# First expert layer of a two-layer network: second products in split f32 instead of f32

## The chip, the cores and the metric

The kernel runs on one core of one Trainium2 chip. The metric is the device time of one execution in microseconds, the median of a few runs. One core has five engines with instruction streams of their own: TensorE (PE; its weight loads are shown as PEld), VectorE (DVE), ScalarE (ACT), GpSimd (POOL) and SyncE (SP, which here only starts DMAs). They order themselves by semaphores.

## The reference

The input is 4 sequences of 1024 rows of 256 numbers, 4096 rows in all. Two layers follow, each an attention-like part and a layer of experts, each added to its input:

```
x = x + L0_attn(layernorm(x))     # gated recurrent scan
x = x + L0_ffn(layernorm(x))      # 8 experts, the best 2 for each row   <- the change is here
x = x + L1_attn(layernorm(x))     # 16 heads, causal softmax
x = x + L1_ffn(layernorm(x))      # 32 experts, the best 4 for each row, and a shared one
```

The first expert layer, for one row x and each of its two experts e, with H = 512:

```
scores = gate_w @ x;  p = softmax(the best two scores)
h1, h2 = w12[e] @ x, split in halves of H
y     += p[e] * (w3[e] @ (silu(h1) * h2))
```

## The kernel before

The program passes four stages: the scan, the first expert layer, the attention, the second expert layer. The change touches the second one.

There, each row has been normalised and written to a DRAM table `routed0` at a place of its expert, so that 128 rows that follow each other there form a tile with one expert. There are TILES0 = 71 tiles at most (4096 x 2 / 128 + 7), and the number of the expert of tile n is found at run time and lies in `b_tei[0, n]`. An engine that needs it for an address reads it into a register first (`value_load`).

The weights of the first products, w12, are held twice: as `b_w12h`, rounded to f32r (a shorter form of f32 that TensorE multiplies in one pass), and `b_w12l`, the rest, also f32r. A product of two such pairs is made as three f32r products (high x high, high x low, low x high) added up in PSUM. The weights of the second products, w3, are held once, in plain f32, for all experts: `b_w3T`.

For tile n the engines do this, in each engine's own order:

- SP (`load_tile`, L655 to L659) loads the tile's rows to `b_xt[j]`, j = n mod 2, once VectorE has made the gates `b_wt` of tile n-2 (s_btk).
- TensorE (`tile_products`) for tile n: `hidden(n, c=0)`, six f32r matmuls with 512 columns into one PSUM bank (L2343 to L2345); `transpose_hidden(n-1)`, four transposes of the gated rows (L2351); `hidden(n, c=1)`, six more; `transpose_rows(n+1)`, two transposes of the next tile's rows (L2332); `second_layer(n-1)`, four f32 matmuls of 128x256, which the trace shows as eight instructions (L2360). So the second products of a tile come one tile late. `hidden(n, 0)` waits for VectorE's low part of the transposed rows (s_btl); `second_layer(n)` for ScalarE's copy of the transposed gated rows (s_bhT) and for the PSUM bank of y (s_bye).
- ScalarE (`tile_step`): `tanh_half(n)` (L1124), `take_hidden(n-1)`, the copy of the gated transposed rows from PSUM (L1128), `take_rows(n+1)`, the high part of the next rows (L1120), `take_y(n-1)`, y times the gate to a ring of four buffers `b_y` (L1137).
- VectorE (`tile_step`): the first gating product (L1726), the second (L1729), `low_rows(n+1)`, the low part of the next rows (L1719), and three small instructions that make the gate (L1737 to L1741).
- GpSimd (`add_rows`): the scatter-add of b_y to DRAM (L888), which waits until the one before has landed.

The order within an engine is fixed by the program; an engine waits at an instruction whose semaphores are not there yet, and all behind it wait too. The next stage starts when all 71 scatter-adds have landed.

Two rows of the trace come from other lines: L1068 and L1571 make `b_w12h` and `b_w12l` (128x1024 at a time) ahead of the tile loop, and L2827 and L2838 are f32r products of the last stage, with 256 columns. L512 is a `value_load` ahead of a DMA (L513), once for each of eight experts, half of them on ScalarE.

Of the kernel before, what the change touches and what calls it, by code (L numbers as in the profile page):

```python
# [5 lines left out]
F32 = mybir.dt.float32  # L6
F32R = mybir.dt.float32r
# [3 lines left out]
ALU = mybir.AluOpType  # L11
ACT = mybir.ActivationFunctionType
AX_X = mybir.AxisListType.X

P = 128
# [30 lines left out]
def network(nc, x_in, a_params, w12T, w3T, gate0T, wqkT, wvT, woT, swT, bias1, ewT, out):  # L46
    B, S, D = x_in.shape
# [3 lines left out]
    E0 = gate0T.shape[2]  # L51
# [10 lines left out]
    KH = H0 // P  # L62
    HT = 2 * H0 // P
    REGION = T + P
    TILES0 = T * K0 // P + E0 - 1
# [20 lines left out]
    with ExitStack() as ctx:  # L86
# [3 lines left out]
        def sem(name):  # L90
            return ctx.enter_context(nc.semaphore(name))
# [28 lines left out]
        def place(name, shape, dt=F32):  # L120
            n = 2 if dt == BF16 else 4
            for s in shape[1:]:
                n *= s
            t = nc.alloc_sbuf_tensor_at(name, shape, dt, offset=at[0])
            at[0] += (n + 31) // 32 * 32
            assert at[0] <= arena_end, (name, at[0] - arena_end)
            return t
# [9 lines left out]
        PS = ctx.enter_context(nc.psum_tensor("PS", [P, 8, 512], F32))  # L137
# [5 lines left out]
        b_w3T = place("b_w3T", [P, KH, E0 * D])  # L143
# [43 lines left out]
        b_tT = [place(f"b_tT{n}", [P, 2, KD, P], F32R) for n in ("_hi", "_lo")]  # L187
        b_sg = place("b_sg", [P, 2, H0])
        b_hid = place("b_hid", [P, 2, H0])
        b_hT = place("b_hT", [P, 2, KH, P])  # L190
        b_y = place("b_y", [P, BY, D])
        b_tok = place("b_tok", [P, BY], U32)
        b_wt = place("b_wt", [P, BY])
# [31 lines left out]
        b_tt = place("b_tt", [P, TILES0])  # L225
        b_tei = place("b_tei", [P, TILES0], I32)
        b_rowi = place("b_rowi", [P, TILES0], I32)

        BLOCKS = [(c, j) for c in range(NC2) for j in range(4 * (c + 1))]
        CHUNKS = [(t, c) for t in range(QT) for c in range(t // 4 + 1)]  # L230
# [147 lines left out]
        s_bhid = sem("b_gated_ready")  # L378
        s_bht = sem("b_gated_transposed")
        s_bhT = sem("b_gatedT_ready")  # L380
        s_by = sem("b_y_ready")
        s_bye = sem("b_y_taken")
        s_xs = sem("x1_stored")
# [139 lines left out]
        def finish_stage(eng, n):  # L523

            leave_stage(eng)
            enter_stage(eng, n)
# [475 lines left out]
        def _(act):  # L1002
# [115 lines left out]
            def take_rows(n, j):  # L1118
                act.wait_ge(s_btt, n + 3)
                act.activation(b_tT[0][:, j, :, :].rearrange("p k t -> p (k t)"), PS[:, 4, 0:D], ACT.Copy).then_inc(s_btT, 1)  # L1120
# [4 lines left out]

            def take_hidden(n, j):
                act.wait_ge(s_bht, n + 1)
                act.activation(b_hT[:, j, :, :].rearrange("p k t -> p (k t)"), PS[:, 5, :], ACT.Copy).then_inc(s_bhT, 1)  # L1128

            def take_y(n, r):  # L1130
                act.wait_ge(s_by, n + 1)
                act.wait_ge(s_btk, n + 3)

                if not (isinstance(n, int) and n < BY):
                    act.wait_ge(s_bst, n * 16 - 16 * (BY - 1))
                act.sem_inc(s_pass, 1)
                act.activation(b_y[:, r, :], PS[:, 6 + r % 2, 0:D], ACT.Identity, bias=zeros[:, 0:1],  # L1137
                               scale=b_wt[:, r:r + 1]).then_inc(s_bye, 1)

            def tile_step(n, r):  # L1140
                tanh_half(n, r % 2)
                take_hidden(n - 1, 1 - r % 2)
                if not (isinstance(n, int) and n == TILES0 - 1):
                    take_rows(n + 1, 1 - r % 2)
                take_y(n - 1, (r - 1) % BY)

            take_rows(0, 0)
            tanh_half(0, 0)
            take_rows(1, 1)
            for n in range(1, BY + 1):  # L1150
                tile_step(n, n % BY)
                if n <= ZERO_PARTS:
                    part = T // ZERO_PARTS
                    act.dma_start(acc[0][(n - 1) * part:n * part, :].rearrange("(q p) d -> p q d", p=P),
                                  zeros[:, :].rearrange("p (a d) -> p a d", a=1).broadcast_to([P, part // P, D])).then_inc(s_dax, 16)
# [327 lines left out]
        def _(dve):  # L1483
# [232 lines left out]
            def low_rows(n, j):  # L1716
# [2 lines left out]
                dve.tensor_tensor(b_tT[1][:, j, :, :].rearrange("p k t -> p (k t)"), PS[:, 4, 0:D],  # L1719
                                  b_tT[0][:, j, :, :].rearrange("p k t -> p (k t)").bitcast(F32), ALU.subtract).then_inc(s_btl, 1)  # L1720

            def tile_step(n, r):
                j = r % 2

                dve.wait_ge(s_bsg, n + 1)
                st.done(dve.scalar_tensor_tensor(b_hid[:, j, :], b_sg[:, j, :], 1.0, PS[:, 2 * j, :], ALU.add, ALU.mult))  # L1726
                st.sync()
                dve.wait_ge(s_bh2, n + 1)
                dve.scalar_tensor_tensor(b_hid[:, j, :], b_hid[:, j, :], 0.5, PS[:, 2 * j + 1, :], ALU.mult,  # L1729
                                         ALU.mult).then_inc(s_bhid, 1)  # L1730
                if not (isinstance(n, int) and n == TILES0 - 1):
                    low_rows(n + 1, 1 - j)

                if not (isinstance(n, int) and n < BY):
                    dve.wait_ge(s_bst, n * 16 - 16 * (BY - 1))
                    dve.sem_inc(s_pass, 1)
                st.done(dve.tensor_copy(b_tok[:, r:r + 1], b_xt[:, j, TOK:TOK + 1].bitcast(U32)))  # L1737
                st.done(dve.tensor_scalar(b_wt[:, r:r + 1], b_xt[:, j, FIRST:FIRST + 1], b_te[:, bass.ds(n, 1)], b_xt[:, j, GAP:GAP + 1],
                                          ALU.is_equal, ALU.mult))
                st.sync()  # L1740
                dve.tensor_tensor(b_wt[:, r:r + 1], b_wt[:, r:r + 1], b_xt[:, j, SECOND:SECOND + 1], ALU.add).then_inc(s_btk, 1)  # L1741
# [10 lines left out]
                st.end()  # L1752
            for n in range((TILES0 // BY - 1) * BY, TILES0):
                tile_step(n, n % BY)
            finish_stage(dve, 1)

            def moments(g):
# [453 lines left out]
        def _(pe):  # L2211
# [111 lines left out]
            def expert_of(n):  # L2323
                return pe.value_load(b_tei[0:1, bass.ds(n, 1)], min_val=0, max_val=E0 - 1)
# [26 lines left out]
                    ins = pe.transpose(PS[:, 5, k * P:(k + 1) * P], b_hid[:, j, k * P:(k + 1) * P], ident[:, :])  # L2351
                ins.then_inc(s_bht, 1)

            def second_layer(n, j, e):
                pe.wait_ge(s_bhT, n + 1)

                pe.wait_ge(s_bye, n + 1)
                pe.sem_inc(s_pass, 1)
                for k in range(KH):
                    ins = pe.matmul(PS[:, 6 + j, 0:D], b_hT[:, j, k, :], b_w3T[:, k, bass.ds(e * D, D)],  # L2360
                                    start=(k == 0), stop=(k == KH - 1))
                ins.then_inc(s_by, 1)

            transpose_rows(0, 0, 0)
            pe.wait_ge(s_wdl, E0 + LO_DVE)
            pe.wait_ge(s_wpl, E0 - LO_DVE)
            pe.wait_ge(s_bw3, 16 * KH)
            e = expert_of(0)
            for c in range(2):
                hidden(0, 0, c, e)  # L2370
# [1 line left out]
            def tile_products(n, half, j):  # L2372
                e = expert_of(n)
                hidden(n, j, 0, e)
                transpose_hidden(n - 1, 1 - j)
                hidden(n, j, 1, e)
                if half:
                    transpose_rows(n + 1, *half, 1 - j)
                second_layer(n - 1, 1 - j, expert_of(n - 1))

            LOOPS = (TILES0 - 2) // 2
            with pe.Fori(0, LOOPS) as i:
# [3 lines left out]
                tile_products(n, ((n + 1) // 2,) if n + 1 < TILES0 else (), n % 2)  # L2386
            last = TILES0 - 1
            transpose_hidden(last, last % 2)
            second_layer(last, last % 2, expert_of(last))
            finish_stage(pe, 1)  # L2390

            pe.sem_inc(s_cPu, 2 * ROUND)
# [522 lines left out]
```

## Time and profile before

| | us |
|---|---|
| median of 3 runs | 2140.64 (2138.8 to 2143.95) |
| the profiled execution: its time | 2142.65 |
| its span in the trace | 2140.9 |
| mean granted clock of TensorE | 0.941 |
| busy: PE / PEld / DVE / ACT / POOL | 1889.4 / 1430.0 / 1361.5 / 1079.1 / 1177.9 |
| the tile loop of this layer, by its first and last tanh | 192.7 to 559.1 |

A row of a group of instructions gives the source line, the engine, the operation, what is written <- what is read, the count, and times. In a timeline the first two numbers are the start and the length in us, and a bracket at the end is the idle time of the engine before it and what ended it. Matmul ends are modelled; weight loads show better when the next matmul is taken up.

### The profile page before, as it was taken

What the parts mean: (1) busy time and instruction counts of PE and PEld (TensorE: products, weight loads), DVE (VectorE), ACT (ScalarE), POOL (GpSimd) and SP (SyncE); (2) the same over time, 40 slices, a digit from 0 to 9 for tenths busy, and PEclk for the clock granted to TensorE, in tenths of its full rate; (3) what the DMA queues carried; (4) which work ended last, traced back from release to release, by engine and by line L of the source; (5) the groups of instructions that cost most, each with busy time, mean ns of one, the idle gap of its engine ahead of it and who ended that gap; (6) DMA issues with size and microseconds to landing.
All of it is one profiled execution on the core that took longest, in us unless ns stands there. A gap on an engine that the chain in (4) does not pass through costs nothing. (4 is left out here: it accounts for less than half of the span.)

```text
span 2140.9 us, 39708 instructions
## 1 busy us (share of the span) xinstructions
PE 1889.4 (88%) x12071; PEld 1430.0 (67%) x12072; DVE 1361.5 (64%) x3652; ACT 1079.1 (50%) x2250; POOL 1177.9 (55%) x1159
## 2 busy tenths in 40 slices
PE   5864999999589999999999999999999999973870
PEld 3553888888466677777777677777777777753750
DVE  7884334434467777657777656777656777653763
ACT  5331333333455556646655646655646655522760
POOL 4364223223216666636687836687836687835782
PEclk9856999999899999999999999999999999977995
DMA  9853433333332111111221111121112111122979
GB/s 335 268 188 119 89 52 49 52 52 49 77 92 56 53 55 49 54 32 53 54 77 41 48 33 53 51 53 47 48 27 59 48 52 51 39 94 70 205 129 257
DMA packets 215682, 177.33 MB, mean 83 GB/s; under 512 B 85442, under 2 KB 200727, under 8 KB 214880
## 3 DMA queue, kind: packets, MB, share of 16 engines
q1 hardware_dynamic: 177904, 138.78, 22.1%
q0 software_dynamic: 28656, 27.61, 8.4%
q10 hardware_dynamic: 8960, 8.92, 1.2%
q8 instruction: 84, 1.38, 0.3%
q14 instruction: 78, 0.64, 0.1%
HBM read 95.05 MB, written 80.72 MB: 82 GB/s over the span
## 5 line engine op out<-in xcount | busy, mean ns | idle before, releaser
L952 POOL TENSOR_TENSOR c_den_late<-c_den_late,c_p 128x512 f32<-128x512 f32 (+3 forms) x384 | 409.9, 1068 | 227.6 <-ACT c_p L1267 183.5
L1267 ACT ACTIVATE c_p<-PS 128x512 f32<-128x512 f32 (+3 forms) x768 | 343.6, 491 | 196.1 <-PE PS L2483 119.0
L2452 PE MATMUL PS<-c_k,c_q 128*128 128x512 f32 (+2 forms) x768 | 289.3, 377 | 18.1 <-DVE c_max L1838 6.7
L2495 PE MATMUL PS<-c_p,c_vh 128*64 128x256 f32 (+3 forms) x3072 | 292.5, 333 | 0.0
L2475 PE MATMUL PS<-c_q,c_k 128*128 128x512 f32 (+2 forms) x768 | 283.7, 373 | 1.8 <-DMA c_q<-c_mr 1.2
L888 POOL DMA_INDIRECT acc<-b_y,b_tok x71 | 110.5, 1557 | 272.8 <-ACT b_y L1137 241.7
L2495 PEld LDWEIGHTS PS<-c_p,c_vh 128*64 128x64 f32 x3072 | 194.6, 137 | 96.0 <-issue 38.1
L2476 PE MATMUL PS<-c_q,c_k 128*128 128x512 f32 (+2 forms) x768 | 258.4, 348 | 0.0
L1258 ACT ACTIVATE c_q<-PS 64x512 fp32r<-64x512 f32 x256 | 151.0, 590 | 208.6 <-PE PS L2439 205.4
L1845 DVE CUSTOM_DVE_ANT_0 PS<-PS,c_maskq,c_max 128x128 f32<-128x128 f32 (+3 forms) x256 | 143.1, 559 | 105.5 <-PE PS L2452 71.5
L1838 DVE TENSOR_REDUCE c_max<-PS 128x1 f32<-128x512 f32 x256 | 175.5, 685 | 54.2 <-PE PS L2452 53.6
L2452 PEld LDWEIGHTS PS<-c_k,c_q 128*128 128x128 f32 x768 | 145.7, 190 | 96.0 <-DVE c_max L1845 40.8
L952 POOL TENSOR_TENSOR c_den<-c_den,c_p 128x384 f32<-128x384 f32 (+2 forms) x192 | 141.5, 737 | 113.7 <-ACT c_p L1267 88.6
L1845 DVE CUSTOM_DVE_ANT_0 PS<-PS,c_maskq 128x128 f32<-128x128 f32 (+3 forms) x256 | 125.9, 501 | 114.5 <-PE PS L2452 109.8
L921 POOL DMA_INDIRECT routed<-r_rows,r_slot x128 | 128.5, 1004 | 60.7 <-DVEq L1956 33.4
L1726 DVE SCALAR_TENSOR_TENSOR b_hid<-b_sg,PS 128x512 f32<-128x512 f32 x71 | 48.9, 689 | 176.1 <-ACT b_sg L1124 176.1
L2475 PEld LDWEIGHTS PS<-c_q,c_k 128*128 128x128 f32 x768 | 145.2, 189 | 16.7 <-DMA c_q<-c_mr 1.3
L2476 PEld LDWEIGHTS PS<-c_q,c_k 128*128 128x128 f32 x768 | 145.1, 189 | 9.0
L2360 PE MATMUL PS<-b_w3T,b_hT 128*128 x568 | 134.8, 380 | 2.7 <-issue 1.7
L2343 PE MATMUL PS<-b_w12h,b_tT_hi 128*128 x284 | 129.2, 455 | 2.3 <-DVE b_tT_lo L1719 2.3
L2522 PE MATMUL PS<-c_wo,c_yT 128*128 128x256 f32 x512 | 124.6, 387 | 0.0
L991 POOL DMA_INDIRECT acc<-d_y,d_tok x64 | 100.5, 1571 | 38.4 <-ACT d_y L1446 20.7
(304 smaller groups left out, 4009.7 us busy)
## 6 DMA issues: line engine op xcount, KB each, us to landing
c_vh<-c_v SPq DMA_DIRECT2D x64, 256.0 KB, 3.2
c_rrow<-rden SPq DMA_DIRECT2D x63, 256.0 KB, 3.6
routed<-b_empty SPq DMA_DIRECT2D x32, 289.0 KB, 10.2
d_xe<-routed SPq DMA_DIRECT2D x32, 289.0 KB, 4.0
b_xt<-routed SPq DMA_DIRECT2D x71, 130.0 KB, 2.1
b_w12T<-in_w12T_dram SPq DMA_DIRECT2D x16, 512.0 KB, 13.9
d_acc<-acc SPq DMA_DIRECT2D x16, 512.0 KB, 9.0
c_st_hi<-wqk_split SPq DMA_DIRECT2D x48, 128.0 KB
```

Of the source, the lines that this page charges most:

```text
L921: pool.indirect_dma_start(routed1, bass.IndirectOffsetOnAxis(ap=r_slot[n][:, j // K1, j % K1:j % K1 + 1], axis=0), r_rows[n][:, j // K1, : ...
L952: pool.tensor_tensor(den[:, off:], den[:, off:], p, ALU.add).then_inc(s_cPa, 1)
L1258: act.activation(dst, src, ACT.Copy).then_inc(s_cqs, 1)
L1267: act.activation(c_p[:, P_AT[h][m]:P_AT[h][m] + WIDTH[m]], PS[:, ST_BANK[m % STB], skip:skip + WIDTH[m]], ACT.Exp, scale=ATT_SCALE).then_i ...
L1838: dve.tensor_reduce(dst, src, AX_X, ALU.max).then_inc(s_turn[bank], 1)
L1845: dve.tensor_tensor_reduce(src, src, c_maskq[:, 512 - w:512], 1.0, dst if c else BIG, ALU.add, ALU.max, dst).then_inc(s_turn[bank], 1)
L2343: pe.matmul(PS[:, 2 * j + c, :], b_tT[0][:, j, k, :], b_w12h[k][:, cols], start=(k == 0), stop=False)
L2360: ins = pe.matmul(PS[:, 6 + j, 0:D], b_hT[:, j, k, :], b_w3T[:, k, bass.ds(e * D, D)], start=(k == 0), stop=(k == KH - 1))
L2452: pe.matmul(PS[:, 2 + use[0], 0:max(w, 256)], c_q1[h][:, t * P:(t + 1) * P], c_k1[h][:, c * 512:c * 512 + max(w, 256)], start=True, stop=T ...
L2475: pe.matmul(PS[:, bank, 0:n], c_k1[h][:, j * P:(j + 1) * P], c_q1[h][:, q], start=True, stop=False)
L2476: ins = pe.matmul(PS[:, bank, 0:n], c_k2[h][:, j * P:(j + 1) * P], c_q2[h][:, q], start=False, stop=not diagonal)
L2495: ins = pe.matmul(dst, c_vh[h][:, j, :], columns[:, :, a, :], start=(j == 0), stop=(t0 == 3))
```

## The change

- A second pair of buffers, `b_w3` (high, low), holds the w3 of one tile's expert in split form; there is one pair, not two. ScalarE makes the high part tile by tile (`high_second`), in its order between `take_rows(n+1)` and `take_y(n-1)`; VectorE makes the low part (`low_second`), at the head of its `tile_step`. Both read the expert's number for themselves.
- The gated transposed rows `b_hT` are split too: ScalarE's copy now rounds to f32r, and VectorE subtracts (`low_hidden`) after its first gating product. There was one f32 buffer for each j; now there is one high and one low for all tiles.
- `second_layer` makes twelve f32r matmuls instead of four f32 ones: eight with the high rows and both weights, then a wait for the low rows, then four with the low rows and the high weights. It no longer reads the expert's number.
- The wait for the loading of w3 moves from TensorE to ScalarE.

```diff
-        b_hT = place("b_hT", [P, 2, KH, P])
+        b_hT = [place(f"b_hT{n}", [P, KH, P], F32R) for n in ("_hi", "_lo")]
...
+        b_w3 = [place(f"b_w3{n}", [P, KH, D], F32R) for n in ("_hi", "_lo")]
...
             def take_hidden(n, j):
                 act.wait_ge(s_bht, n + 1)
-                act.activation(b_hT[:, j, :, :].rearrange("p k t -> p (k t)"), PS[:, 5, :], ACT.Copy).then_inc(s_bhT, 1)
+                act.activation(b_hT[0][:, :, :].rearrange("p k t -> p (k t)"), PS[:, 5, :], ACT.Copy).then_inc(s_bhT, 1)
+
+            def high_second(n):
+
+                if not (isinstance(n, int) and n == 0):
+                    act.wait_ge(s_by, n)
+                e = act.value_load(b_tei[0:1, bass.ds(n, 1)], min_val=0, max_val=E0 - 1)
+                act.activation(b_w3[0][:, :, :], b_w3T[:, :, bass.ds(e * D, D)], ACT.Copy).then_inc(s_w3h, 1)
...
                     take_rows(n + 1, 1 - r % 2)
+                high_second(n)
                 take_y(n - 1, (r - 1) % BY)

+            act.wait_ge(s_bplan, 2)
+            act.wait_ge(s_bw3, 16 * KH)
             take_rows(0, 0)
             tanh_half(0, 0)
             take_rows(1, 1)
+            high_second(0)
...
+            def low_second(n):
+
+                dve.wait_ge(s_w3h, n + 1)
+                e = dve.value_load(b_tei[0:1, bass.ds(n, 1)], min_val=0, max_val=E0 - 1)
+                dve.tensor_tensor(b_w3[1][:, :, :], b_w3T[:, :, bass.ds(e * D, D)], b_w3[0][:, :, :].bitcast(F32),
+                                  ALU.subtract).then_inc(s_w3l, 1)
+
+            def low_hidden(n):
+
+                dve.wait_ge(s_bhT, n + 1)
+                dve.tensor_tensor(b_hT[1][:, :, :].rearrange("p k t -> p (k t)"), PS[:, 5, :],
+                                  b_hT[0][:, :, :].rearrange("p k t -> p (k t)").bitcast(F32), ALU.subtract).then_inc(s_bhl, 1)
+
             def tile_step(n, r):
                 j = r % 2

+                if not (isinstance(n, int) and n == 0):
+                    low_second(n - 1)
                 dve.wait_ge(s_bsg, n + 1)
                 st.done(dve.scalar_tensor_tensor(b_hid[:, j, :], b_sg[:, j, :], 1.0, PS[:, 2 * j, :], ALU.add, ALU.mult))
+                if not (isinstance(n, int) and n == 0):
+                    low_hidden(n - 1)
                 st.sync()
...
-            def second_layer(n, j, e):
+            def second_layer(n, j):
                 pe.wait_ge(s_bhT, n + 1)
+                pe.wait_ge(s_w3l, n + 1)

                 pe.wait_ge(s_bye, n + 1)
                 pe.sem_inc(s_pass, 1)
                 for k in range(KH):
-                    ins = pe.matmul(PS[:, 6 + j, 0:D], b_hT[:, j, k, :], b_w3T[:, k, bass.ds(e * D, D)],
-                                    start=(k == 0), stop=(k == KH - 1))
+                    for w in range(2):
+                        pe.matmul(PS[:, 6 + j, 0:D], b_hT[0][:, k, :], b_w3[w][:, k, :], start=(k == 0 and w == 0), stop=False)
+                pe.wait_ge(s_bhl, n + 1)
+                for k in range(KH):
+                    ins = pe.matmul(PS[:, 6 + j, 0:D], b_hT[1][:, k, :], b_w3[0][:, k, :], start=False, stop=(k == KH - 1))
                 ins.then_inc(s_by, 1)
```

## Rows read from the trace of the kernel before

**Rows 1.** Stretches in us: busy by engine (instructions), granted clock, DMA share, GB/s.
```profile
core 0: us, PE busy (x) PEld busy (x) DVE busy (x) ACT busy (x) POOL busy (x), PEclk, DMA share, GB/s
120.00:180.00 60.00, 25.07 (x167) 22.59 (x167) 48.96 (x232) 19.80 (x25) 40.43 (x38) 0.50 0.43 147
...
400.00:500.00 100.00, 100.00 (x504) 83.18 (x503) 41.22 (x118) 39.07 (x77) 29.80 (x20) 1.00 0.33 51
2040.00:2060.00 20.00, 16.66 (x96) 12.97 (x95) 13.13 (x39) 13.85 (x31) 16.61 (x12) 0.91 0.89 180
2060.00:2080.00 20.00, 15.83 (x112) 13.82 (x110) 15.09 (x43) 14.25 (x33) 16.90 (x11) 1.00 0.65 73
```

**Rows 2.** Waits from 200 to 560 us: who <- whom, us in total, times, longest.
```profile
DVE b_hid L1726 <- ACT b_sg L1124: 170.0, 69, 3.6
...
PEld PS L2343 <- issue: 3.9, 18, 0.2
```

**Rows 3.** Timeline of one tile in the loop, all engines, some lines of it.
```profile
401.95 0.19 PEld L2343 LDWEIGHTS PS<-b_w12h,b_tT_hi 128*128 128x128 f32 x1
...
403.32 0.59 PEld L2351 LDWEIGHTS PS<-ident,b_hid 128*128 128x128 f32 x4
...
403.75 0.60 ACT L1124 ACTIVATE b_sg<-PS 128x512 f32<-128x512 f32 x1 [0.65 <-PE PS L2345]
...
403.87 0.19 PEld L2343 LDWEIGHTS PS<-b_w12h,b_tT_hi 128*128 128x128 f32 x1
...
404.38 0.69 DVE L1726 SCALAR_TENSOR_TENSOR b_hid<-b_sg,PS 128x512 f32<-128x512 f32 x1 [2.42 <-ACT b_sg L1124]
...
405.48 1.60 PEld L2360 LDWEIGHTS PS<-b_w3T,b_hT 128*128 128x128 f32 x8
...
405.76 0.69 DVE L1729 SCALAR_TENSOR_TENSOR b_hid<-b_hid,PS 128x512 f32<-128x512 f32 x1 [0.69 <-PE PS L2345]
...
406.36 0.42 DVE L1719 TENSOR_TENSOR b_tT_lo<-PS,b_tT_hi 128x256 fp32r<-128x256 f32 x1
...
407.21 0.19 PEld L2343 LDWEIGHTS PS<-b_w12h,b_tT_hi 128*128 128x128 f32 x1
...
407.68 0.57 ACT L1137 ACTIVATE b_y<-PS,zeros,b_wt 128x256 f32<-128x256 f32 x1 [1.51 <-DMA acc<-b_y,b_tok]
```

**Rows 4.** The tanh's line: ns min/median/max, first and last start.
```profile
L1124 ACT ACTIVATE b_sg<-PS x71: 597/597/599, 192.7 to 559.1; 128x512 f32<-128x512 f32 x71
```

**Rows 5.** Timeline of PE alone, last stage, around two groups of L2838.
```profile
2062.57 0.28 PE L2838 MATMUL PS<-d_wf,d_eh_lo 128*128 128x256 f32 x1
...
2062.81 0.28 PE L2838 MATMUL PS<-d_wf,d_eh_lo 128*128 128x256 f32 x1
...
2065.01 0.39 PE L2838 MATMUL PS<-d_wf,d_eh_hi 128*128 128x256 f32 x1 [0.53 <-DVE d_eh_lo L2184]
...
2065.47 0.28 PE L2838 MATMUL PS<-d_wf,d_eh_lo 128*128 128x256 f32 x1
```

**Rows 6.** Lines that do such conversions elsewhere: ns min/median/max, first and last start.
```profile
L1068 ACT ACTIVATE b_w12h<-b_w12T x16: 1039/1043/1047, 126.2 to 157.8; 128x1024 fp32r<-128x1024 f32 x16
...
L1571 DVE TENSOR_TENSOR b_w12l<-b_w12T,b_w12h x14: 1217/1224/1226, 128.1 to 174.7; 128x1024 fp32r<-128x1024 f32 x14
...
L1808 DVE TENSOR_TENSOR c_xT_lo<-PS,c_xT_hi x16: 680/692/693, 588.5 to 1547.5; 128x512 fp32r<-128x512 f32 x16
```

**Rows 7.** Register reads on ScalarE's queue and the DMA issues behind them, same columns.
```profile
L512 ACTq TENSOR_LOAD <-b_zrowi x4: 279/382/542, 159.9 to 163.4; - x4
...
L512 ACTq FUSED_REGOPS  x4: 152/157/170, 160.4 to 164.0; - x4
...
L513 ACTq DMA_DIRECT2D routed<-b_tail x4: 343/353/451, 160.8 to 164.3; - x4
```

**Rows 8.** The page's DMA issues (KB, us to landing), and the last scatter-adds in GpSimd's timeline.
```profile
b_xt<-routed SPq DMA_DIRECT2D x71, 130.0 KB, 2.1
...
565.06 1.55 POOL L888 DMA_INDIRECT acc<-b_y,b_tok  x1 [4.23 <-DMA acc<-b_y,b_tok]
569.71 1.55 POOL L888 DMA_INDIRECT acc<-b_y,b_tok  x1 [3.10 <-DMA acc<-b_y,b_tok]
```

More of the change, by code:

```diff
@@ L380, in network @@
         s_bhT = sem("b_gatedT_ready")
+        s_bhl = sem("b_gatedT_lo_ready")
+        s_w3h = sem("b_second_weights_hi_ready")
+        s_w3l = sem("b_second_weights_lo_ready")
         s_by = sem("b_y_ready")
@@ L1754, in _ @@
                 tile_step(n, n % BY)
+            low_second(TILES0 - 1)
+            low_hidden(TILES0 - 1)
             finish_stage(dve, 1)
@@ L2366, in _ @@
             pe.wait_ge(s_wpl, E0 - LO_DVE)
-            pe.wait_ge(s_bw3, 16 * KH)
             e = expert_of(0)
@@ L2378, in tile_products @@
                     transpose_rows(n + 1, *half, 1 - j)
-                second_layer(n - 1, 1 - j, expert_of(n - 1))
+                second_layer(n - 1, 1 - j)
             LOOPS = (TILES0 - 2) // 2
@@ L2388, in _ @@
             transpose_hidden(last, last % 2)
-            second_layer(last, last % 2, expert_of(last))
+            second_layer(last, last % 2)
             finish_stage(pe, 1)
```

## The prediction

> **What bounds the kernel now.** I read the table by stretches first. In the tile loop of the first expert layer TensorE is busy 100.00 of 100.00 us (400 to 500) at a granted clock of 1.00, VectorE 41%, ScalarE 39%, GpSimd 30% [rows 1]. A busy PE can still be a waiting one, because the ends of matmuls are modelled, so next come the waits: in 360 us PE's own largest wait there is 3.9 us of "issue", while VectorE waits 170.0 us for ScalarE's tanh, which itself waits for PE's products [rows 2]. Last the timeline of one tile [rows 3], where the starts of the weight loads (PEld) give PE's true pace: 1.37 us for the six products of a first half (401.95 to 403.32), 0.55 for four transposes, 1.61 for the second half and two transposes of the next rows, and 1.73 for the eight matmuls of the second layer (405.48 to 407.21), together 5.26 us with no hole. The line of the tanh gives the mean period: 71 starts from 192.7 to 559.1, so 366.4/70 = 5.23 us [rows 4]. PE's instruction stream bounds this stage: what shortens the stream is worth its full size times 71, until something else is late.
>
> **Part one: the products.** Eight f32 matmuls (four blocks, each two instructions) become twelve in f32r of the same 128x256. The last stage of this kernel has this very kind of product, f32r halves of 256 columns at clock 1.00: they start every 0.12 us (2062.57, then 2062.81 two on) [rows 5]. 12 x 0.12 = 1.44 us against 1.73: 0.29 us less per tile. PE would need 5.26 - 0.29 = 4.97 us, or 4.94 beside the mean period. It also drops one of its two reads of the expert's number per tile, which now lie under matmuls: nothing.
>
> **Part two: new work beside PE.** ScalarE gets a copy of 128x1024 to f32r from on-chip memory; the same copy takes 1.043 us in L1068. VectorE gets a subtraction of 128x1024, 1.224 us in L1571, and one of 128x512 out of PSUM, 0.69 us in L1808 [rows 6]. As load that would fit: in 5.23 us ScalarE works 0.39 x 5.23 = 2.0, then 3.1; VectorE 2.2, then 4.1. Neither is the bound by its sum. What matters is order.
>
> **Part three: the waits added.** The split pair b_w3 has one buffer. So high_second(n) waits until y(n-1) has been computed, and y(n) waits for the split. Between the two nothing overlaps: the change makes a ring, and its round is the tile's period if it is longer than PE's stream. I add it up from the end of y(n-1):
>
> 1. ScalarE sees the end, reads the expert's number into a register and starts the copy. The trace shows such a read on this engine four times: the load takes 0.279 to 0.542 us, the register operations behind it 0.157, and from the first load to the first DMA issue that uses it 0.9 us pass (159.9 to 160.8), from the last one too (163.4 to 164.3) [rows 7]. With the median load of 0.382, not 0.54, it is 0.75. A hop between engines costs 0.03 (the tanh ends at 403.75 + 0.60 = 404.35, VectorE starts at 404.38) [rows 3]. I take 0.80 in all. The bounds: nothing, if the sequencer could do it ahead of the wait (it stands behind the wait in program order, which speaks against), and 1.17, the spacing of those four loads with a DMA issue in between (3.5/3).
> 2. The copy: 1.04. Sum 1.84.
> 3. VectorE: low_second waits for the copy and then reads the number itself: 0.80 again, same bounds. Sum 2.64.
> 4. Its subtraction: 1.22, but the next instruction may start about 0.08 before the end (L1729 and L1719 start 0.60 apart, the first being 0.69 long) [rows 3]: 1.14. Sum 3.78.
> 5. Behind it in VectorE's queue stands the first gating product of tile n+1: 0.61. Sum 4.39. Its input, the tanh, stands behind the copy and take_y(n-1) on ScalarE: 1.84 + 0.57 + 0.60 = 3.0, in time [rows 3].
> 6. low_hidden(n), the low part of the gated rows: 0.69. Sum 5.08. The high part is ready at about 3.6.
> 7. PE's last four matmuls wait for it: in the last stage four such after a wait on VectorE run from 2065.01 to 2065.47 + 0.28 = 2065.75, so 0.74, and 0.04 for the hop [rows 5]. Sum 5.86 us, and y(n) is done.
>
> The first eight products can start when the low weights are there (3.86) and end before 5.08: hidden. PE's stream of the next tile is late next: low_rows(n+2) ends at 5.08 + 0.61 + 0.38 = 6.07, PE starts the next tile there, 0.21 after y(n), and reaches the second layer 3.53 later, at 3.74 of its round, 0.12 before the weights. So the ring decides, narrowly ahead of PE's own way.
>
> Other edits and movements: take_y(n-1) now stands behind the copy on ScalarE, so the scatter-add on GpSimd starts some 1.9 us later in its round. Its own chain, each add waiting for the landing of the one before, can run at 4.65 us (565.06 to 569.71, where only the landing held it) [rows 8]; below 5.86, so it costs nothing but would hold a faster loop. SP's load of tile n+2 waits for VectorE's b_wt, later by as much as the round: its rows land 2.1 us after issue [rows 8], and PE asks for them about 3.2 us (12 products of 0.23 and four transposes) after starting a tile; covered by about half a microsecond, and if not, PE waits that much, most of it under the ring. The waits for the plan and the weights, moved ahead of the loop on ScalarE, are over by then: zero. Outside this stage nothing changes; the stages behind it start later by the same amount, since the next one needs the sums of all scatter-adds.
>
> **The sum.** 5.86 against 5.23: 0.63 x 70 = 44 us, plus the last tile, which has no next tile on PE beside it: its y follows the one before after 5.25 us of the ring (5.86 less step 5) instead of about 3 (transposes 0.55, a copy of some 0.6, matmuls 1.73), +2. So 46 us. The profiled run took 2142.65 us (span 2140.9 and 1.75 around it), which gives 2188.7; it lies 2.0 above the median of 2140.64, so on the scale of the medians I forecast 2187.
>
> For the size of a register read there is a stated figure. The trace has loads of 0.279 to 0.542 us, and 0.9 until the value is used [rows 7]. The Trainium skill, "DMA: Bandwidth & Descriptors", section "Latency and other measured facts", puts the floor of a `tensor_load` at about 600 ns; an estimate with 0.6 in place of both 0.80 gives 5.46 us a round and 2159 us.
>
> **The rivals.**
> - PE stays the bound, the kernel gets faster. The conversions would have to fit beside the stream. The ring falls below 5.23 when the two reads together cost under 0.97 us instead of 1.60; with reads of no cost it is 4.26, and PE's 4.94 decides: 0.29 x 71 = 21 us less, 2120. For it: PE is the bound now without doubt, and both engines are under half busy [rows 1]. Against it: the wait stands ahead of the read in both queues. 8%.
> - The ring just equals the old period, between 5.17 and 5.29: no difference. 3%.
> - The reads are dear on these engines, 1.17 each: 6.60 us a round, 1.37 x 70 = 96, 2237. The upper ends of the loads speak for a piece of that, their median against. 8%.
> - The clock falls. PE now idles about 0.9 us in 5.86. In 120 to 180 us, where it was busy 25.07 of 60, it was granted 0.50; in the last stage 16.66 of 20 us went with 0.91 and 15.83 of 20 with 1.00 [rows 1]. PE will be busy 4.94/5.86 = 84%, as there. At half speed its stream takes 9.9 us; if a tenth of the tiles ran so, 7 x 4.0 = 28 us more, 2215. 4%.
>
> "TensorE: Matmul & The Clock Gate" of the Trainium skill, section "HAM oscillation — how this bites in real kernels", says that frequent small idle times of TensorE can make its clock swing between the two levels; the stretches of the last stage, with such holes, show 0.91 and 1.00, so it is borne out a little.
>
> **Numbers.** Forecast, a ring of 5.4 to 6.3 us: 77%. Its own range is what reads of 0.6 to 1.0 us give: 5.46 (+16 to +18) to 6.26 (+74), so 2158 to 2215. Outside lie the faster case with the even one (11%) and the dear end; I set 2157 to 2218. A difference of under 0.2% (4 us) can't be told from none here. Slower: 77 + 8 + 4 = 89, less 1 for a ring that falls short: 88%. Same 3%, faster 9%.
>
> **What would show it.** Right: the second layer's products in twelve, 0.12 us apart, with a PE wait before them for VectorE (low weights) and before the last four (low gated rows); the copy on ScalarE waiting for PE each tile; a period near 5.9 of the tanh; PE under 90% in the loop. Step 1 or 3 is wrong if from the end of y to the copy, or from the copy to the subtraction, much other than 0.8 us pass. The whole is wrong if PE stays at 100% there, or if the clock leaves 1.00.

## The result, and the profile after

The changed kernel takes 2201.89 us (median of 4 runs, 2196.72 to 2203.03), the kernel before 2139.78 on the same chip (4 runs): a ratio of 1.028, 95% interval 1.026 to 1.029; the medians are 62 us apart. The forecast was 2187, with a range of 2157 to 2218. By their own profiled executions the two are 2201.86 and 2142.65, a difference of 59.2 us.

A stretch of the tile loop, in the columns of [rows 1]:

```profile
400.00:500.00 100.00, 89.47 (x499) 72.23 (x497) 63.69 (x136) 47.75 (x82) 38.62 (x17) 1.00 0.28 43
```

TensorE fell from 100% to 89%, VectorE rose from 41% to 64%, ScalarE from 39% to 48%; the clock stayed at 1.00. No engine is full any more: that is the look of a ring of waits. Its stations are in the list of waits from 240 to 600 us, about 60 tiles, against [rows 2]:

```profile
DVE b_w_lo L1741 <- ACT b_w_hi L1139: 131.4, 59, 2.3
ACT b_w_hi L1139 <- PE PS L2399: 131.1, 60, 2.6
...
PEld PS L2377 <- issue: 48.7, 60, 1.1
PE PS L2377 <- DVE b_tT_lo L1734: 36.8, 60, 0.9
...
PEld PS L2399 <- DVE b_hT_lo L1747: 5.2, 30, 0.2
```

ScalarE's copy waits in every tile for the last products of the tile before (L2399), VectorE's subtraction in every tile for the copy. In the timeline (start, length) one round can be followed line by line, against [rows 3]:

```profile
408.38 0.74 PE L2399 MATMUL PS<-b_w_hi,b_hT_lo 128*128 128x256 f32 x4
408.84 0.41 DVE L1734 TENSOR_TENSOR b_tT_lo<-PS,b_tT_hi 128x256 fp32r<-128x256 f32 x1
...
409.54 0.19 PEld L2377 LDWEIGHTS PS<-b_w12h,b_tT_hi 128*128 128x128 f32 x1 [0.62 <-issue]
...
410.02 1.06 ACT L1139 ACTIVATE b_w_hi<-b_w3T 128x1024 fp32r x1 [2.02 <-PE PS L2399]
...
411.95 1.23 DVE L1741 TENSOR_TENSOR b_w_lo<-b_w3T,b_w_hi 128x1024 fp32r<-128x1024 f32 x1 [2.25 <-ACT b_w_hi L1139]
```

y ends at 408.38 + 0.74 = 409.12; the copy starts at 410.02, 0.90 later, and ends at 411.08; the subtraction starts 0.87 later, at 411.95. The rest of the same round:

```profile
413.09 0.68 DVE L1756 SCALAR_TENSOR_TENSOR b_hid<-b_sg,PS 128x512 f32<-128x512 f32 x1
413.69 0.68 DVE L1747 TENSOR_TENSOR b_hT_lo<-PS,b_hT_hi 128x512 fp32r<-128x512 f32 x1
414.42 0.74 PE L2399 MATMUL PS<-b_w_hi,b_hT_lo 128*128 128x256 f32 x4
```

So y ends next at 415.16: a round of 6.04 us. The tanh gives the mean, against [rows 4], and three lines with the register reads stand against [rows 7]:

```profile
L1128 ACT ACTIVATE b_sg<-PS x71: 585/597/602, 193.6 to 615.9; 128x512 f32<-128x512 f32 x71
...
L1138 ACTq TENSOR_LOAD <-b_tei x71: 275/428/510, 196.5 to 619.6; - x71
...
L1740 DVEq TENSOR_LOAD <-b_tei x71: 299/305/1062, 198.3 to 621.8; - x71
...
L2358 PEldq TENSOR_LOAD <-b_tei x71: 298/308/491, 188.9 to 612.9; - x71
```

422.3/70 = 6.03 us a tile against 5.23: 0.80 x 70 = 56 us, and the other 3 of the 59.2 us are lost at the two ends of the loop.

### The profile page after: what moved, and what is told of

Same layout as the page of the kernel before. It is cut to its first block and busy times, and to the rows that moved or that the text cites. A ratio compares the mean times of both kernels' runs of the same rounds, so it can differ in the third digit from the quotient of the medians.

```text
span 2200.1 us, 40735 instructions
## 1 busy us (share of the span) xinstructions
PE 1906.8 (87%) x12355; PEld 1433.6 (65%) x12356; DVE 1478.7 (67%) x3795; ACT 1143.3 (52%) x2322; POOL 1224.2 (56%) x1159
## 5 line engine op out<-in xcount | busy, mean ns | idle before, releaser
L892 POOL DMA_INDIRECT acc<-b_y,b_tok x71 | 155.8, 2194 | 285.4 <-ACT b_y L1148 269.2
L1741 DVE TENSOR_TENSOR b_w_lo<-b_w3T,b_w_hi 128x1024 fp32r<-128x1024 f32 x71 | 87.0, 1225 | 159.9 <-ACT b_w_hi L1139 144.8
L1139 ACT ACTIVATE b_w_hi<-b_w3T 128x1024 fp32r x71 | 75.3, 1060 | 155.9 <-PE PS L2399 151.9
```

The costliest lines, as they stand in the source:

```text
L892: pool.indirect_dma_start(acc0, bass.IndirectOffsetOnAxis(ap=b_tok[:, r:r + 1], axis=0), b_y[:, r, :], None, compute_op=ALU.add).then_inc( ...
```

## The experiments

The runs of this section were made on three chips, on which the kernel before takes 2141.2, 2155.5 and 2156.2 us, so ratios to the kernel before are compared. The theory: the ring y, read, copy, read, subtraction, gating, low rows, last products. The rivals: the load of VectorE and ScalarE as such; the late start of TensorE's tiles; the new products themselves.

**Both reads ahead of their waits.** The number of the expert doesn't depend on what the two engines wait for.

```diff
             def high_second(n):
-                if not (isinstance(n, int) and n == 0):
-                    act.wait_ge(s_by, n)
                 e = act.value_load(b_tei[0:1, bass.ds(n, 1)], min_val=0, max_val=E0 - 1)
+                if not (isinstance(n, int) and n == 0):
+                    act.wait_ge(s_by, n)
             def low_second(n):
-                dve.wait_ge(s_w3h, n + 1)
                 e = dve.value_load(b_tei[0:1, bass.ds(n, 1)], min_val=0, max_val=E0 - 1)
+                dve.wait_ge(s_w3h, n + 1)
```

> The changed kernel, with the register reads of the expert's number on ScalarE and VectorE each put ahead of the wait behind which they stood; nothing else differs. Ring theory: in the changed kernel's trace the round of 6.03 us contains 0.92 us from the end of y to the copy on ScalarE and 0.84 us from the copy to the subtraction on VectorE, nearly all of it the two reads. With the reads in waiting time the ring falls to about 4.4 us, PE's own stream decides at 4.95 to 5.25 us a tile, and the time is 2125 to 2150, so not slower than the kernel before (2139.8). Load theory (VectorE and ScalarE simply have more to do, or TensorE's starts are late because of the low rows): where the reads stand makes no difference, 2195 to 2203.

Measured: 2139.56 us, ratio 0.999 (0.998 to 1.000). Moving two lines gives back the whole loss, as expected. In its timeline:

```profile
402.43 0.54 PEld L2399 LDWEIGHTS PS<-b_w_hi,b_hT_lo 128*128 128x128 f32 x4
402.95 0.19 PEld L2377 LDWEIGHTS PS<-b_w12h,b_tT_hi 128*128 128x128 f32 x1
403.31 1.06 ACT L1139 ACTIVATE b_w_hi<-b_w3T 128x1024 fp32r x1 [1.13 <-PE PS L2399]
...
404.52 1.23 DVE L1741 TENSOR_TENSOR b_w_lo<-b_w3T,b_w_hi 128x1024 fp32r<-128x1024 f32 x1 [1.41 <-ACT b_w_hi L1139]
...
407.34 0.54 PEld L2399 LDWEIGHTS PS<-b_w_hi,b_hT_lo 128*128 128x128 f32 x4
...
408.58 0.19 PEld L2377 LDWEIGHTS PS<-b_w12h,b_tT_hi 128*128 128x128 f32 x1 [0.69 <-issue]
```

With 0.74 for the last products, y ends at about 403.17; the copy follows after 0.14 instead of 0.90, the subtraction after 0.15 (404.37 to 404.52) instead of 0.87. The reads were nearly all of these two gaps. The load theory is out: both engines do the same work in less time. And a new thing shows: every second tile TensorE begins 1.24 us after the start of the last four weight loads, not 0.52.

**One read at a time.** The same edit on one engine alone.

> The changed kernel with only ScalarE's read ahead of its wait. Ring theory: 6.03 - 0.85 = 5.2 us a tile, 58 us less than the changed kernel, 2140 to 2150. Load theory: 2195 to 2203.

> The changed kernel with only VectorE's read ahead of its wait. Ring theory: 6.03 - 0.78 = 5.25 us a tile, 55 us less than the changed kernel, 2142 to 2152. Load theory: 2195 to 2203. If only one of this run and the one with ScalarE's read gains, that side alone was the late one and there is no ring.

Measured: 2172.32 us, ratio 1.014 (1.012 to 1.016), and 2162.18 us, ratio 1.009 (1.008 to 1.011). Both gain, so there is a ring through both engines, but 0.014 and 0.019 below the changed kernel's 1.028 are only 30 and 40 us, half to three quarters of the 58 and 55 that were expected. Both expectations missed. The waits of the first of the two from 240 to 560 us point at TensorE:

```profile
PEld PS L2377 <- issue: 28.9, 29, 1.1
PE PS L2377 <- DVE b_tT_lo L1734: 23.1, 29, 0.9
```

29 waits in 57 tiles, 1 us each: in every second tile TensorE is late with its own start. The expectations had left TensorE's own way out. Whether it makes up the whole of the missing 28 and 15 us was not tested by itself.

**The suspected cost doubled.**

```diff
+                act.value_load(b_tei[0:1, bass.ds(n, 1)], min_val=0, max_val=E0 - 1)
                 e = act.value_load(b_tei[0:1, bass.ds(n, 1)], min_val=0, max_val=E0 - 1)
```

> The changed kernel with the read on ScalarE made twice in a row behind its wait, the first one's value not used: the suspected cost doubled on one side. ScalarE is busy only half the time. Ring theory: the second read lengthens the round by the 0.5 to 0.8 us that a read takes, 35 to 56 us more than the changed kernel, 2237 to 2258. Load theory: ScalarE hides it, 2200 to 2206.

Measured: 2236.45 us, ratio 1.044 (1.042 to 1.046): 0.016, some 34 us, or 0.5 us a tile, on an engine that is busy 44% of the time. This is the low end of what was expected (2237). The second of the two reads in a row is a load of 0.278 us at the median, with 0.152 and 0.018 of register work behind it:

```profile
L1139 ACTq TENSOR_LOAD <-b_tei x71: 272/278/287, 193.7 to 654.3; - x71
```

**TensorE's read and branch ahead.** In the changed kernel TensorE starts a tile 0.42 us (409.12 to 409.54) after y, every second one 0.8 after:

```profile
402.36 0.73 PE L2399 MATMUL PS<-b_w_hi,b_hT_lo 128*128 128x256 f32 x4
...
403.87 0.19 PEld L2377 LDWEIGHTS PS<-b_w12h,b_tT_hi 128*128 128x128 f32 x1 [0.98 <-issue]
```

If this late start were the loss, putting the read and the branch ahead of the second layer should give it back. The matmuls keep their order; the loop is cut at another place.

```diff
             def tile_products(n, half, j):
                 e = expert_of(n)
+                if not (isinstance(n, int) and n == 1):
+                    second_layer(n - 2, j)
                 hidden(n, j, 0, e)
...
                     transpose_rows(n + 1, *half, 1 - j)
-                second_layer(n - 1, 1 - j)
```

> The changed kernel with only TensorE's read and branch ahead of the second layer; the reads on ScalarE and VectorE stay behind their waits. TensorE waits 0.4 to 0.8 us at the start of each tile in the changed kernel. Ring theory: that wait lies under the ring, which does not pass through it; 6.0 us a tile as before, 2196 to 2205. Rival (the late start of TensorE's tile is the loss): 0.6 us a tile less, about 2160.

Measured: 2214.30 us against 2155.5, ratio 1.027 (1.025 to 1.029): nothing, as the ring theory expected. The trace shows that the edit took away only a part of the late start:

```profile
401.02 0.42 DVE L1734 TENSOR_TENSOR b_tT_lo<-PS,b_tT_hi 128x256 fp32r<-128x256 f32 x1
401.72 0.19 PEld L2377 LDWEIGHTS PS<-b_w12h,b_tT_hi 128*128 128x128 f32 x1 [0.50 <-issue]
...
407.04 0.42 DVE L1734 TENSOR_TENSOR b_tT_lo<-PS,b_tT_hi 128x256 fp32r<-128x256 f32 x1
407.74 0.19 PEld L2377 LDWEIGHTS PS<-b_w12h,b_tT_hi 128*128 128x128 f32 x1 [0.63 <-issue]
```

Here every tile starts 0.28 to 0.29 us after VectorE has ended the low part of the next rows (L1734), which is 0.3 to 0.4 after y. In the changed kernel the tiles that start at 0.42 have the same 0.28 to 0.29 (408.84 + 0.41 = 409.25, start at 409.54), and the others 0.60 to 0.73. TensorE's queue shows what is different in those, for the tiles that start at 409.54 and at 416.02:

```profile
L2358 PEldq TENSOR_LOAD <-b_tei x2: 307/340/373, 408.5 to 415.0; - x2
...
L2358 PEldq SEQ_ASSERT  x2: 18/18/18, 409.1 to 415.6; - x2
...
L2419 PEldq COMPARE_BRANCH  x1: 207/207/207, 414.5 to 414.5; - x1
```

Without the branch the read is over at 409.1, before the low part of the next rows, so the read costs nothing and those rows decide. With the branch ahead of it the read is over at 415.6, later than the rows (414.88 + 0.41 = 415.29). So the late start has two causes: the next rows in all tiles, and branch and read on top in every second one. Only the second was removed here, about 0.2 us a tile on average, which would be some 13 us or a ratio of 1.022 if it counted. The late start lies under the ring, as long as there is one.

**All three reads ahead.**

> The kernel of the run with both reads ahead, and on TensorE the read of the next tile's expert number and the loop's branch put ahead of the second layer's products (the same matmuls in the same order; only the loop is cut at another place). In that run's trace every other tile starts on TensorE about 0.5 us after y instead of 0.2 before its end, because the wait for the low gated rows holds the sequencer, and the branch and the read come behind it (about 1.3 us after the low rows, 1.6 with the branch). If that is so, these tiles lose nothing now: about 0.3 us a tile on average, 4.9 to 5.0 us, 2114 to 2124, faster than the kernel before by about 1%. If the late start is due to the low part of the next rows instead, nothing changes: 2136 to 2143.

Measured: 2167.01 us against 2155.5, ratio 1.005 (1.003 to 1.006): not the gain of 1%, but worse than with two reads ahead. TensorE's weight loads in its timeline:

```profile
403.74 0.38 PEld L2366 LDWEIGHTS PS<-ident,b_xt 128*128 128x128 f32 x2
404.08 0.19 PEld L2396 LDWEIGHTS PS<-b_w_hi,b_hT_hi 128*128 128x128 f32 x1
...
405.91 0.19 PEld L2377 LDWEIGHTS PS<-b_w12h,b_tT_hi 128*128 128x128 f32 x1 [0.34 <-issue]
...
409.01 0.37 PEld L2366 LDWEIGHTS PS<-ident,b_xt 128*128 128x128 f32 x2
409.87 0.19 PEld L2396 LDWEIGHTS PS<-b_w_hi,b_hT_hi 128*128 128x128 f32 x1 [0.49 <-issue]
```

Without the branch the second layer follows the transposes by 0.34, with it by 0.86. Branch and read had only changed their place: where they stand now a read is covered, but not a read and a branch. And at 405.91 TensorE waited for the low part of the next rows (VectorE's L1734 ended at 405.21 + 0.41 = 405.62, 0.29 before), though the profile books it as "issue". So each of the two causes that the expectation had as rivals was half of it.

**No tile by tile split.** The weights of expert 0 are split once ahead of the loop.

```diff
-                high_second(n)
                 take_y(n - 1, (r - 1) % BY)
...
-                if not (isinstance(n, int) and n == 0):
+                if isinstance(n, int) and n == 1:
                     low_second(n - 1)
```

> The changed kernel without the tile by tile split of the second weights: those of expert 0 are split once ahead of the loop and used for all tiles (so the part left out is the other experts' second weights, and the output differs). The twelve f32r products and the split of the gated rows stay. Ring theory: no wait of this kind is left, TensorE's stream decides at 4.95 us plus the exposed branch and read on every other tile, 5.0 to 5.25 a tile, 2120 to 2141. Rival (twelve products instead of eight, or the low gated rows, cost the time): the time stays above 2180. GpSimd's scatter-adds take 2.27 us in the changed kernel instead of 1.555; if VectorE's subtraction from and to on-chip memory beside them is the reason, they are back at 1.56 here.

Measured: 2148.72 us against 2155.5, ratio 0.996 (0.995 to 0.997). The twelve products and the split of the gated rows are no loss: the rival is out. Its tanh runs from 207.3 to 566.7, 5.13 us a tile. That mean holds one odd tile at the start, which this edit makes by itself: TensorE waits there for the one split.

```profile
212.60 1.23 DVE L1740 TENSOR_TENSOR b_w_lo<-b_w3T,b_w_hi 128x1024 fp32r<-128x1024 f32 x1 [1.46 <-issue]
...
215.08 0.29 PEld L2375 LDWEIGHTS PS<-b_w12h,b_tT_hi 128*128 128x128 f32 x1 [5.54 <-issue]
```

From the first tanh to the second 10.74 us pass, and behind that wait the granted clock was 0.72 over 216 to 222, so the lower level for a part of it. Soon after, the tiles take 4.9 and 5.14 to 5.26 in turn. And the scatter-adds are short again (changed kernel first, then this run):

```profile
L892 POOL DMA_INDIRECT acc<-b_y,b_tok x71: 1555/2270/2566, 205.7 to 628.4; - x71
```

```profile
L892 POOL DMA_INDIRECT acc<-b_y,b_tok x71: 1555/1555/1627, 223.7 to 576.1; - x71
```

**Two buffers for the high weights.** Another way to open the ring, with the reads left where they were.

```diff
-                if not (isinstance(n, int) and n == 0):
-                    act.wait_ge(s_by, n)
+                if not (isinstance(n, int) and n <= 1):
+                    act.wait_ge(s_by, n - 1)
...
                 dve.wait_ge(s_w3h, n + 1)
+                if not (isinstance(n, int) and n == 0):
+                    dve.wait_ge(s_by, n)
```

> The changed kernel with two buffers for the high part of the split weights (the low part keeps one); ScalarE's copy for tile n now waits for y(n-2), VectorE's subtraction for the copy and for y(n-1). No read is moved. Ring theory: the first 1.95 us of the round (ScalarE's read and copy) fall out, the rest of it is 4.1 us, TensorE decides with its exposed read and branch: 5.2 to 5.5 us a tile, 2135 to 2160. Rival (where the buffers are doesn't matter, the load does): 2195 to 2205.

Measured: 2161.75 us against 2155.5, ratio 1.003 (1.002 to 1.004), which is 2146 on the scale of the expectation (2139.8). The copy is off the ring and nearly all of the loss is gone. Two buffers for both parts were not tried.

**The low gated rows first on VectorE.**

```diff
                     low_second(n - 1)
+                    low_hidden(n - 1)
                 dve.wait_ge(s_bsg, n + 1)
                 st.done(dve.scalar_tensor_tensor(b_hid[:, j, :], b_sg[:, j, :], 1.0, PS[:, 2 * j, :], ALU.add, ALU.mult))
-                if not (isinstance(n, int) and n == 0):
-                    low_hidden(n - 1)
```

> The changed kernel with one order changed on VectorE: the low part of the gated rows (low_hidden) right behind the subtraction of the weights, ahead of the first gating product of the next tile. Simple reading of the ring: the gating product (0.6 us) leaves it, 5.4 us a tile, ratio to the kernel before about 1.008. Ring theory with TensorE's own way close behind it: all that VectorE does up to the low part of the next rows ends no earlier (6.14 us after y in the changed kernel's trace), TensorE starts 0.29 later, needs 3.44 to the second layer and 1.7 for it, 11.57 us for two tiles, 5.8 a tile: ratio 1.018 to 1.024. The changed kernel has 1.028.

Measured: 2206.02 us against 2156.2, ratio 1.023 (1.022 to 1.025). The second way of reckoning holds: to take one station out of a ring gives only as much as the next path, here over the low part of the next rows, lies behind it. In its trace every tile of TensorE starts 0.28 to 0.29 us after the low part of the next rows.

**All cures together, and the controls.** Two buffers for the high weights, all reads ahead, and twelve tiles in a round of TensorE's loop; the same with one pair of buffers; and the kernel before with this loop.

```diff
-            LOOPS = (TILES0 - 2) // 2
+            UNROLL = 12
+            LOOPS = (TILES0 - 3) // UNROLL
+            tile_products(1, (1,), 1)
             with pe.Fori(0, LOOPS) as i:
-                for j in (1, 0):
-                    tile_products(i * 2 + (2 - j), (i + 1,), j)
+                for m in range(UNROLL):
+                    tile_products(i * UNROLL + (2 + m), (i * (UNROLL // 2) + (3 + m) // 2,), m % 2)
```

> The changed kernel with two buffers for the high weights, the reads on ScalarE and VectorE ahead of their waits, and TensorE's read and branch ahead of the second layer with twelve tiles in a loop's round instead of two. If nothing but the twelve shorter products is left to act, TensorE needs 4.86 to 4.95 us a tile against 5.19 to 5.23: 20 to 25 us less than the kernel before, ratio 0.988 to 0.991. If another bound is near (the chain of scatter-adds at 4.65, or VectorE, whose work is 4.3 us of 4.9), 5.0 to 5.2, ratio 0.993 to 1.000.

> As the run with all three reads ahead, still one pair of weight buffers, but twelve tiles in a round of TensorE's loop. That run had 5.77 and 4.83 us for alternate tiles; the long one holds the branch and the read, 1.3 us of sequencer time that the short products no longer cover. If that is the cause, nearly all tiles are short, limited at 4.98 to 5.1 us by the low part of the next rows (4.69 us after y, and 0.29 until TensorE starts): ratio 0.991 to 0.997. If the long tile has another cause, 5.3 us stays: 1.003 to 1.006.

> The kernel before (f32 second products) with the same cut of TensorE's loop and twelve tiles in a round: how much of a gain comes from the loop and not from the products. Its loop-back tiles lose 0.1 to 0.2 us now: at most 0.1 us a tile, ratio 0.996 to 1.000. If the loop were the whole gain, this kernel would equal the best of the others.

Measured: all cures 2142.74 us against 2156.2, ratio 0.994 (0.992 to 0.995), faster than both kernels. One pair: 1.000 (0.999 to 1.001). The kernel before with this loop: 1.010 (1.008 to 1.012), slower. The timeline of the first has the period that was looked for (starts of a tile's tanh):

```profile
427.18 0.60 ACT L1130 ACTIVATE b_sg<-PS 128x512 f32<-128x512 f32 x1 [0.58 <-PE PS L2383]
...
432.06 0.60 ACT L1130 ACTIVATE b_sg<-PS 128x512 f32<-128x512 f32 x1 [0.61 <-PE PS L2383]
```

That is 4.9 us a tile, the forecast of PE's stream alone (4.94 to 4.97). The mean over the loop is more, 5.07 (207.9 to 562.6): about 12 us are lost in ten of the 70 steps. So the time lies in the expectation's second case (0.993 to 1.000), but not by a slower steady tile, as that case has it. The largest losses, 3.8 and 1.5 us, begin with waits for the loading of the rows, and each turn of the loop costs 0.4 to 0.5:

```profile
232.16 0.20 PEld L2370 LDWEIGHTS PS<-ident,b_xt 128*128 128x128 f32 x2 [1.70 <-DMA b_xt<-routed]
...
269.56 0.20 PEld L2370 LDWEIGHTS PS<-ident,b_xt 128*128 128x128 f32 x2 [0.79 <-DMA b_xt<-routed]
...
340.23 0.19 PEld L2400 LDWEIGHTS PS<-b_w_hi,b_hT_hi 128*128 128x128 f32 x1 [0.44 <-issue]
```

```profile
230.00:234.00 4.00, 2.13 (x13) 1.40 (x12) 2.52 (x7) 1.00 (x3) 1.21 (x1) 1.00 0.92 261
234.00:238.00 4.00, 4.00 (x18) 3.31 (x17) 1.23 (x1) 1.36 (x3) 1.17 (x1) 0.57 0.56 183
```

The first of these waits fell in a stretch with a DMA share of 0.92 (0.34 in 300 to 500). Behind it the granted clock was 0.57 in 234 to 238, with the lower of the two levels, 0.50, from 235 to 237: the clock did leave 1.00 once here. What the first tiles and the last ones lose besides was not settled.

In the run with one pair every second tile waits for the low part of the next rows:

```profile
410.89 0.41 DVE L1734 TENSOR_TENSOR b_tT_lo<-PS,b_tT_hi 128x256 fp32r<-128x256 f32 x1
411.59 0.19 PEld L2377 LDWEIGHTS PS<-b_w12h,b_tT_hi 128*128 128x128 f32 x1 [0.33 <-issue]
```

This again is 0.29 from its end to TensorE's start, as its expectation has it; its mean, 5.19 (208.7 to 572.2), is above the 5.1 expected, with slow tiles at the start and at the turns of the loop too. Its ratio of 1.000 lies between the expectation's two cases (0.991 to 0.997 and 1.003 to 1.006): a miss. And the kernel before with the new cut puts two reads in a row (the tile's expert and the one of two tiles before); every second tile its second layer comes late:

```profile
404.91 0.37 PEld L2332 LDWEIGHTS PS<-ident,b_xt 128*128 128x128 f32 x2
405.65 1.59 PEld L2360 LDWEIGHTS PS<-b_w3T,b_hT 128*128 128x128 f32 x8 [0.37 <-issue]
```

0.74 from one to the other, where the kernel before has 0.34 (its transposes' loads start at 405.14, the second layer's at 405.48, [rows 3]). That expectation missed: it took the cut to be free. So this run is no fair control for the loop: it adds a cost that the kernel before doesn't have. The tanh of the kernel before gives an estimate instead:

```profile
388.19 0.60 ACT L1124 ACTIVATE b_sg<-PS 128x512 f32<-128x512 f32 x1 [0.67 <-PE PS L2345]
...
393.35 0.60 ACT L1124 ACTIVATE b_sg<-PS 128x512 f32<-128x512 f32 x1 [0.57 <-PE PS L2345]
...
398.61 0.60 ACT L1124 ACTIVATE b_sg<-PS 128x512 f32<-128x512 f32 x1 [0.68 <-PE PS L2345]
```

Tile by tile its steps are 5.14 to 5.17 us (388.19 to 393.35), and every fourth 5.24 to 5.28 (393.35 to 398.61). If that 0.1 in four tiles is what its loop of two tiles costs, a longer loop gives it 2 us or 0.1%, and the run with all cures gains 0.6% (0.5 to 0.8). So by this estimate nearly all of the gain comes from the shorter products. The kernel before with its own order and a longer loop was not run.

## Why the prediction was right, and where it was off

- What bounds the kernel before (PE's stream): right. Without the ring, the shorter products bring the loop to 4.9 us a tile.
- Part one, 0.12 us a product: right. The first eight start 0.12 apart in the run with both reads ahead. With the split once for all a gain of 0.4% (7 us) is left of 0.29 x 71 = 21 us (1.0%). Of the missing 14, the odd first tile of that run takes 5.8 (10.74 less 4.90), and the branch and the read, below, take about 0.27 in every second tile, some 9.
- Part two, the load is not the bound: right. In the run with both reads ahead the same work is done in 5.24 us a tile (tanh from 194.7 to 561.5).
- Part three, the ring: right in every station, and not by errors that cancel. By steps, forecast and measured: 1, hop, read and start on ScalarE, 0.80 and 0.90; 2, the copy, 1.04 and 1.06; 3, the same read on VectorE, 0.80 and 0.87; 4, subtraction, 1.14 and 1.14; 5, gating, 0.61 and 0.60; 6, low gated rows, 0.69 and 0.68; 7, hop and last products, 0.78 and 0.79. Sum 5.86 and 6.04. The mis-sized term is the read, 0.10 and 0.07 short; over 70 tiles the whole 0.17 is 12 of the 13 us by which the measured difference (59.2) exceeds the forecast one (46). On ScalarE the load took 0.428 at the median, where the forecast had taken 0.382. The 0.9 from load to use that [rows 7] showed was nearer as it stood than the 0.75 that the forecast made of it.
- The bound of "nothing" for a read: a read costs nothing only if it stands ahead of the wait; behind it, as here, it costs all of itself. The figure of the Trainium skill ("DMA: Bandwidth & Descriptors", "Latency and other measured facts", about 600 ns) gives 5.46 us for the round, which is under the measured 6.04; the load alone is shorter here (0.3 to 0.43), and the whole gap with hop, register work and start is longer (0.9).
- Wrong, in two terms: "PE starts the next tile there, 0.21 after y(n)". The start is 0.42 after y in one tile and 0.8 in the next. First, the low part of the next rows ends 0.13 after y, earlier than forecast, but TensorE starts 0.28 to 0.29 behind that end, and the forecast had nothing for this step. Second, the forecast priced TensorE's remaining read at nothing and did not count the loop's branch. The wait for the low gated rows stands in the middle of the second layer and holds TensorE's sequencer; read and branch come only behind it. The read alone is over before the next rows are ready and does cost nothing; with the branch, in every second tile, it costs 0.3 to 0.45. In the changed kernel the ring hides both, as the run with only TensorE's read moved shows (1.027) for the second.
- The step "0.12 before the weights", so narrowly under the ring: right in one tile of two. TensorE needs 3.44 from its start to the second layer. The tiles that start at 0.42 are there 0.20 before the weights (409.54 + 3.44 = 412.98, the subtraction ends at 413.18); the others 0.17 after them (407.31 against 407.14), and are still in time for the low gated rows, by about 0.1. So the ring decides everywhere, but barely. That it came out so near is in part luck: both TensorE's start and the weights were forecast too early. The order on VectorE, tried alone, gave 0.005 where its 0.6 us would have been 0.020.
- The scatter-adds: the chain was to cost nothing at 5.86, and it did; but each took 2.27 us instead of 1.56, which the forecast didn't have.
- The clock stayed at 1.00 in the loop with TensorE at 89%, so that rival did not come. The Trainium skill tells of a clock that swings with frequent small idle times ("TensorE: Matmul & The Clock Gate", under "A second HAM failure mode: psum-queue depth-cycling", not under the heading that the prediction names). The changed kernel's trace, with TensorE's waits of 0.4 to 1.1 us in every tile, does not show such a swing; the run with all cures shows the lower level once, behind waits of 1.70 and 0.82 us.

## What to carry to other kernels

When new work is put between two uses of one buffer on engines that are half idle, add up the way round from the last reader to the next reader before adding up the load: here 4.5 us of work and 1.5 us of register reads made a ring of 6.0 us while no engine was over 90%. Put a register read ahead of the wait whenever its value doesn't depend on it; of two such moves one alone gave back half of the loss, the other two thirds, both together all of it. When a stage is shortened, look for the path that lies next behind the one removed: here it was TensorE's start behind the low part of the next rows, and each single cure gave less than its own length because of what lay close behind the ring. And a wait in the middle of an engine's instructions also delays the reads and branches behind it, so what used to lie under long instructions has to be counted again once they are shorter.

## What the runs showed of the hardware

- A read of a register from on-chip memory behind a wait costs 0.7 to 0.8 us here until the dependent instruction starts (0.90 against 0.14 on ScalarE, 0.87 against 0.15 on VectorE). The load itself is 0.3 to 0.43 of that. A second read right behind the first costs 0.5.
- GpSimd's indirect DMA instruction takes 2.27 us instead of 1.56 when it starts while VectorE subtracts two operands in on-chip memory: in the changed kernel it started at 412.30, the subtraction ran from 411.95 to 413.18, and of that 0.88 was left. Over the adds of the changed kernel and of the runs with two buffers, the added time is what is left of the subtraction at the add's start, less about 0.13 (0.84 left: 0.72 more; 0.38 left: 0.25 more). Where the add starts near the subtraction's end, as in the run with both reads ahead (1.58 us), or where there is no subtraction, it is back at its old length.
- A register read between two groups of TensorE's products did not show (0.34 us from one group's loads to the next), a read and the loop's branch showed as 0.5 us more (0.86; 0.82 at the turn of the loop with twelve tiles), two reads as 0.4 more (0.74). The reading, an inference from these, is that TensorE's sequencer runs only some tenths of a microsecond ahead of the array.
- From the end of VectorE's low part of the next rows to TensorE's start 0.28 to 0.29 us pass in the tiles that wait for it: every tile of the run with only TensorE's read moved and of the run with the other order on VectorE, every second one of the changed kernel. Behind the low gated rows it is 0.05 (413.69 + 0.68 to 414.42). What makes the difference was not tested.
